# A convolution stage of a four-layer kernel: third block as a split product, statistics on ScalarE, filters' low parts spread through DRAM

## The reference

```
x = x + conv(layernorm(x), k, skip, ctx, ctx, heads=8)
x = x + experts(layernorm(x))          # 8 experts, top 2, and a shared one
x = x + attention(layernorm(x), ctx, ...)
x = x + dense(layernorm(x))
```

## Time and profile before

| | us |
|---|---|
| median of 3 runs (lowest, highest) | 3148.43 (3147.88, 3150.55) |
| the profiled execution | 3145.92 |
| its span in the trace | 3143.3 |
| PE busy in the span | 3092.0 (98%) |
| VectorE / ScalarE / GpSimd busy | 2204.3 / 1216.9 / 1154.9 |
| DMA traffic | 277.67 MB, mean 88 GB/s |

### The profile page before, as it was taken

The page is one execution under the profiler, slowest core; times in us unless marked ns, Lnnn a source line. Parts: engine busy times, 40 slices in busy tenths (PEclk is TensorE's granted clock), DMA queues, the critical chain, the costliest instruction groups (busy, mean ns, idle before and its releaser), DMA issues.

```text
span 3143.3 us, 49423 instructions
## 1 busy us (share of the span) xinstructions
PE 3092.0 (98%) x18229; PEld 2652.6 (84%) x18229; DVE 2204.3 (70%) x5733; ACT 1216.9 (39%) x2883; POOL 1154.9 (37%) x1176
## 2 busy tenths in 40 slices
PE   8999999999999899999999999999999999999999
PEld 5767676799899689999999999999998888888887
DVE  7999999755555688888888888888888433333342
ACT  3333333333444355555555555555555311111111
POOL 8988887545344332222222222222201011000010
PEclk9999999999999999999999999999999999999999
DMA  4434432279777721111111111111101200000000
GB/s 142 144 121 141 128 111 81 90 262 317 215 228 227 243 75 55 48 48 45 44 48 48 48 48 42 40 48 40 43 28 57 88 27 27 27 27 27 27 14 14
DMA packets 124973, 277.67 MB, mean 88 GB/s; under 512 B 18312, under 2 KB 18960, under 8 KB 124736
## 3 DMA queue, kind: packets, MB, share of 16 engines
q1 hardware_dynamic: 95712, 178.54, 18.0%
q0 software_dynamic: 29024, 95.97, 9.3%
HBM read 170.04 MB, written 104.42 MB: 87 GB/s over the span
## 4 chain that ended last, share of the span: by engine, by line
PE 92%; DVE 6%; DMA 1%; POOL 1%; ACT 1%; issue 0%; SPq 0%; POOLq 0%; DVEq 0%
PE f_Y L513 4%; PE g_PH L2426 4%; PE g_PH L2428 4%; PE g_PH L2427 4%; PE g_O L2442 4%; PE g_O L2441 4%; PE g_O L2440 4%; PE t_U L1704 4%; PE t_U L1705 4%; PE t_U L1706 4%; PE t_T L1680 3%; PE f_Y L519 3%; PE f_Y L521 3%; PE f_Y L518 3%; PE t_PO L1690 2%; PE t_S L1669 2%
## 5 line engine op out<-in xcount | busy, mean ns | idle before, releaser
L1830 ACT ACTIVATE t_pr<-t_sm,t_nb 128x256 f32<-128x256 f32 x512 | 256.6, 502 | 408.3 <-DVE t_nb L2037 408.3
L2211 POOL TENSOR_TENSOR t_r<-t_r 128x256 f32<-128x256 f32 x128 | 94.4, 737 | 730.7 <-DVE t_r L2016 412.7
L2498 DVE CAST g_hh<-g_hf 128x512 fp32r<-128x512 f32 x128 | 54.6, 427 | 431.0 <-PE g_O L2442 429.4
L1259 POOL TENSOR_TENSOR c_kf<-c_vt,c_ct 128x512 f32<-128x512 f32 x256 | 296.0, 1172 | 9.0 <-PE f_Y L513 9.0
L2469 ACT ACTIVATE g_hf<-g_PH,b1g 128x512 f32<-128x512 f32 x128 | 88.2, 689 | 493.8 <-PE g_PH L2428 493.8
L2047 DVE TENSOR_SCALAR t_pr<-t_pr,t_rw 128x256 f32<-128x256 f32 x512 | 239.1, 467 | 18.1
L518 PE MATMUL f_Y<-c_kh,c_th 128*128 128x512 f32 x448 | 224.5, 501 | 4.2 <-DVE c_z L976 2.6
L1704 PE MATMUL t_U<-t_voh,t_oth 128*128 128x512 f32 x512 | 202.3, 395 | 0.0
L2426 PE MATMUL g_PH<-g_xh,g_w 128*128 128x512 f32 x512 | 202.0, 395 | 0.0
L1705 PE MATMUL t_U<-t_voh,t_otl 128*128 128x512 f32 x512 | 201.6, 394 | 0.0
L1706 PE MATMUL t_U<-t_vol,t_oth 128*128 128x512 f32 x512 | 200.4, 391 | 0.0
(11 more groups left out here) (334 smaller groups left out, 9784.6 us busy)
## 6 DMA issues: line engine op xcount, KB each, us to landing
xs<-c_zero SPq DMA_DIRECT2D x71, 256.0 KB, 4.5
f_xg<-xs SPq DMA_DIRECT2D x71, 256.0 KB, 3.5
ys<-f_yt POOLq DMA_DIRECT2D x71, 256.0 KB, 3.7
f_xg<-xn SPq DMA_DIRECT2D x40, 256.0 KB, 4.9
c_xt<-x SPq DMA_DIRECT2D x32, 256.0 KB, 3.5
c_cr<-ctx SPq DMA_DIRECT2D x32, 256.0 KB, 3.9
c_ct<-ctxh SPq DMA_DIRECT2D x32, 256.0 KB, 4.4
c_t<-kt SPq DMA_DIRECT2D x32, 256.0 KB, 4.8
```

Source lines behind the costliest of these rows:

```text
L1259: gp.tensor_tensor(o, iv, ic, ALU.mult).then_inc(*GP("kv", n))
```

## The change

In words:

- Block mb = 2 is split like 0 and 1 (`if mb > 2`), so 4 plain products a head become 12 fp32r ones. Its high part is a ScalarE copy; its low part is VectorE's for u = 0 and GpSimd's for u = 1 (`low_by`).
- Statistics of both norms move from VectorE to ScalarE from head 2 on (rows of the second norm: all but the last): a Copy pass with scale -1/512 and an accumulator gives minus the mean, a Square pass with that as bias and an accumulator gives the variance; two small ones add epsilon and make the shift. Both tiles' roots lie side by side in `rsb`, and one GpSimd power serves both (`powers`).
- The filter's low part `tl` of heads 2 to 31 is no longer subtracted on GpSimd. All 32 filters (32 x 512) are loaded once (`kq`), split once into `khi` and `klo` (with 128 zeros ahead), and eight DMAs, one in each of heads 0 to 7, write 4 filters each, 128 times repeated at a pitch of 641, to DRAM (`tlt`). Read at a pitch of 640 that is the Toeplitz matrix; `load` fetches it (`tlf`), and ScalarE copies it to `tl` (`filter_lo`).
- `turned_rows`, `norm_rows`, `logit` and `best` of a head move some steps later; at the end of the loop those of head 30 move behind it. `store_xn` moves from (u=1, lb=2) of head h+1 to (u=0, lb=3) of head h+2.
- The constant `mhalf` has two columns instead of one.

The core of the diff:

```diff
@@ sync_front
+    tlw = d["tlt"].rearrange("h (p c) -> h p c", c=641)[:, :, 0:640]
+    tlr = d["tlt"][:, 128:].rearrange("h (p c) -> h p c", c=640)[:, :, 0:512]
@@ load(h)
+        if h > 1:
+            w.wait_ge(*AC["tl", h - 2 if h > 3 else -1])
+            w.wait_ge(*Q["kw"]["tlt", h // 4])
+            sp.dma_start(m.tlf[:, h % 2, :], tlr[h]).then_inc(*Q[f"u{h % 2}"]("tlf", h))
+
+    def spread_filters(c):
+        w.wait_ge(*VE["klo"])
+        w.wait_ge(*Q["kw"]["tlt", c - 1])
+        r = slice(4 * c, 4 * c + 4)
+        sp.dma_start(tlw[r], m.klo[r, :].unsqueeze(1).to_broadcast([4, 128, 640])).then_inc(*Q["kw"]("tlt", c))
...
+                if u == 0 and lb == 1 and h < 8:
+                    spread_filters(h)
                 if u == 0 and lb == 2 and h + 2 < NHC:
                     load(h + 2)
@@ conv
-            if mb > 1:
+            if mb > 2:
@@ scalar_front
+    def filters_hi():
+        w.wait_ge(*Q["kw"]["kq"])
+        copy(m.khi[:, :], m.kq[:, :]).then_inc(*AC("khi"))
+
+    def filter_lo(h):
+        w.wait_ge(*Q[f"u{h % 2}"]["tlf", h])
+        w.wait_ge(*PE["y", 8 * (h - 2) + 7])
+        copy(m.tl[:, h % 2, :], m.tlf[:, h % 2, :]).then_inc(*AC("tl", h))
+
+    def mean(h):
+        s = h % 2
+        w.wait_ge(*Q[f"x{h % 4}"]["x", h])
...
+        ac.activation(m.xn[:, s, :], m.xt[:, h % 4, :], ACT.Copy, scale=-1.0 / D, accum_out=m.ag[:, s, 0:1]).then_inc(*AC("mean", h))
+
+    def spread(h):
+        s = h % 2
+        w.wait_ge(*AC["mean", h])
+        ac.activation(m.xn[:, s, :], m.xt[:, h % 4, :], ACT.Square, bias=m.ag[:, s, 0:1], accum_out=m.ag[:, s, 1:2]).then_inc(*AC("ba", h))
+        w.wait_ge(*AC["ba", h])
+        ac.activation(root(m, h), m.ag[:, s, 1:2], ACT.Copy, scale=1.0 / D, bias=EPS).then_inc(*AC("var", h))
...
+    def mean_rows(i):
+        s = i % 2
+        w.wait_ge(*VE["out2", i])
...
@@ the loop of scalar_front, in the order of the calls within a step
                 if u == 1 and lb == 0 and more:
                     filter_hi(h + 1)
+                if u == 1 and lb == 0 and h:
+                    mean_rows(h - 1)
+                if u == 0 and lb == 0 and h and more:
+                    shift(h + 1)
                 if u == 0 and lb == 0 and more:
                     norm(h + 1)
-                if u == 0 and lb == 0 and h > 1:
-                    turned_rows(h - 2)
...
                     split(*UNITS[n])
...
+                if u == 1 and lb == 1 and h:
+                    spread_rows(h - 1)
+                if u == 1 and lb == 1 and h + 2 < NHC:
+                    mean(h + 2)
+                if u == 1 and lb == 2 and h + 2 < NHC:
+                    spread(h + 2)
+                if u == 0 and lb == 0 and h > 1:
+                    shift_rows(h - 2)
+                    norm_rows(h - 2)
                 if u == 0 and lb == 2 and h > 1:
+                    turned_rows(h - 2)
+                if u == 0 and lb == 3 and 1 <= h < LAST:
+                    filter_lo(h + 1)
+                if u == 1 and lb == 0 and h > 1:
                     logit(h - 2)
@@ vector_front
+    def filters_lo():
+        ve.memset(m.klo[:, 0:128], 0.0).then_inc(*VE("klo0"))
+        w.wait_ge(*AC["khi"])
+        ve.tensor_tensor(m.klo[:, 128:640], m.kq[:, :], f32(m.khi[:, :]), ALU.subtract).then_inc(*VE("klo"))
...
     low(0, 0, 0)
     skips(0)
+    low(0, 0, 2)
+    filters_lo()
...
-                if u == 1 and lb == 2 and h + 2 < NHC:
-                    stats(h + 2)
...
-                gather_i(h, u, lb, UNITS[n] if n < len(UNITS) and lb == 0 else None)
+                gather_i(h, u, lb, UNITS[n] if n < len(UNITS) and (lb == 0 or (lb == 2 and u)) else None)
...
-                if h and u == 1 and lb == 0:
-                    stats_rows(h - 1)
@@ gpsimd_front
+    def powers(h):
+
+        w.wait_ge(*AC["var", h + 2])
+        w.wait_ge(*AC["var0", h - 1])
+        gp.tensor_tensor(m.rsb[:, h % 2, :], m.rsb[:, h % 2, :], mhalf, ALU.pow).then_inc(*GP("rs", h + 2))
...
+                if u == 1 and lb == 3 and h < LAST:
+                    if h == 0:
+                        power(2)
+                    elif h + 2 < NHC:
+                        powers(h)
...
-                if u == 0 and lb == 1:
+                if u == 0 and lb in (1, 2):
                     low(*UNITS[n])
-                if u == 1 and lb == 0 and more:
-                    filter_lo(h + 1)
+                if u == 1 and lb == 0 and h == 0:
+                    filter_lo(1)
```

More of the change, by code:

```diff
@@ L177, in front_memory @@
     m.ob = c("ob", [8, 2, 512])
-    c("pad", [128, 3688])
+    m.tlf = c("tlf", [128, 2, 512])
+    m.khi = c("khi", [NHC, 512], F32R)
+    c("pad", [128, 104])
     sw = c("sw", [128, 8192], F32R)
@@ L342, in turn_at, with root, root_rows, filter_by @@
     return None
+def root(m, h):
+    return m.rsb[:, h % 2, 0:1]
+def root_rows(m, i):
+    return m.rsb[:, (i + 1) % 2, 1:2]
+def filter_by(K, h):
+    return K.VE if h == 0 else K.GP if h == 1 else K.AC
+def low_by(K, u, mb):
+    return K.VE if mb == 0 or (mb == 2 and u == 0) else K.GP
 def sync_front(sp, w, K):
@@ L433, in sync_front @@
                     stage_shared(h)
-                if u == 1 and lb == 2 and h:
+                if u == 0 and lb == 3 and h > 1:
+                    store_xn(h - 2)
+                if u == 1 and lb == 3 and h == LAST:
                     store_xn(h - 1)
@@ L515, in conv @@
             w.wait_ge(*AC["th", h])
-            w.wait_ge(*(GP if h else VE)["tl", h])
+            w.wait_ge(*filter_by(K, h)["tl", h])
             w.wait_ge(*AC["kh", n])
@@ L519, in conv @@
             pe.matmul(Y, m.tl[:, s, c], m.kh[:, v, mb, :], start=False, stop=False)
-            w.wait_ge(*(GP if mb else VE)["kl", n])
+            w.wait_ge(*low_by(K, u, mb)["kl", n])
             t = pe.matmul(Y, m.th[:, s, c], m.kl[:, v, mb, :], start=False, stop=mb == lb)
@@ L654, in tensor_front @@
             turn_out(LAST)
+            turn_rows(LAST - 1)
+        if n == 2:
             logit(LAST - 1)
@@ L748, in filter_hi @@
         copy(m.th[:, s, :], m.t[:, h % 3, :]).then_inc(*AC("th", h))
+    def filters_hi():
[8 more added lines that the diff above has]
+        w.wait_ge(*Q[f"x{h % 4}"]["x", h])
+        w.wait_ge(*(VE if h < 4 else AC)["nm", h - 2])
+        w.wait_ge(*VE["w", h - 2])
+        w.wait_ge(*PE["pv", h - 2])
+        w.wait_ge(*AC["xn", h - 2])
+        ac.activation(m.xn[:, s, :], m.xt[:, h % 4, :], ACT.Copy, scale=-1.0 / D, accum_out=m.ag[:, s, 0:1]).then_inc(*AC("mean", h))
@@ new lines, in spread, with shift @@
+    def spread(h):
[4 more added lines that the diff above has]
+        ac.activation(root(m, h), m.ag[:, s, 1:2], ACT.Copy, scale=1.0 / D, bias=EPS).then_inc(*AC("var", h))
+    def shift(h):
+        s = h % 2
+        w.wait_ge(*GP["rs", h])
+        ac.activation(m.nm[:, s, :], m.ag[:, s, 0:1], ACT.Copy, scale=root(m, h)).then_inc(*AC("nm", h))
@@ new lines, in mean_rows, with spread_rows @@
+    def mean_rows(i):
+        s = i % 2
+        w.wait_ge(*VE["out2", i])
+        w.wait_ge(*AC["xb", i - 2])
+        w.wait_ge(*PE["px", i - 2])
+        w.wait_ge(*Q[f"n{s}"]["nd", i - 2])
+        ac.activation(m.xb[:, s, :], m.xt[:, i % 4, :], ACT.Copy, scale=-1.0 / D, accum_out=m.ag0[:, s, 0:1]).then_inc(*AC("mean0", i))
+    def spread_rows(i):
+        s = i % 2
+        w.wait_ge(*AC["mean0", i])
+        ac.activation(m.xb[:, s, :], m.xt[:, i % 4, :], ACT.Square, bias=m.ag0[:, s, 0:1], accum_out=m.ag0[:, s, 1:2]).then_inc(*AC("ba0", i))
+        w.wait_ge(*AC["ba0", i])
+        ac.activation(root_rows(m, i), m.ag0[:, s, 1:2], ACT.Copy, scale=1.0 / D, bias=EPS).then_inc(*AC("var0", i))
@@ L750, in norm, with shift_rows @@
+    def shift_rows(i):
+        s = i % 2
+        w.wait_ge(*(GP["rs", i + 3] if i + 3 < NHC else GP["rs0", i]))
+        ac.activation(m.nm0[:, s, :], m.ag0[:, s, 0:1], ACT.Copy, scale=root_rows(m, i)).then_inc(*AC("nm0", i))
     def norm(h):
         s = h % 2
-        w.wait_ge(*VE["nm", h])
+        w.wait_ge(*(VE if h < 2 else AC)["nm", h])
         w.wait_ge(*VE["w", h - 2])
         w.wait_ge(*PE["pv", h - 2])
-        ac.activation(m.xn[:, s, :], m.xt[:, h % 4, :], ACT.Identity, scale=m.rs[:, s, :], bias=m.nm[:, s, :]).then_inc(*AC("xn", h))
+        ac.activation(m.xn[:, s, :], m.xt[:, h % 4, :], ACT.Identity, scale=root(m, h), bias=m.nm[:, s, :]).then_inc(*AC("xn", h))
@@ L790, in norm_rows @@
         s = i % 2
-        w.wait_ge(*VE["nm0", i])
+        w.wait_ge(*(VE if i == LAST else AC)["nm0", i])
         w.wait_ge(*PE["px", i - 2])
         w.wait_ge(*Q[f"n{s}"]["nd", i - 2])
-        ac.activation(m.xb[:, s, :], m.xt[:, i % 4, :], ACT.Identity, scale=m.rs0[:, s, :], bias=m.nm0[:, s, :]).then_inc(*AC("xb", i))
+        ac.activation(m.xb[:, s, :], m.xt[:, i % 4, :], ACT.Identity, scale=root_rows(m, i), bias=m.nm0[:, s, :]).then_inc(*AC("xb", i))
     def turned_rows(i):
@@ L811, in scalar_front @@
         split(*UNITS[n])
+    filters_hi()
```

(18 more changed lines are left out.)

64 lines of the change are left out of this document (28 added, 36 removed).

## The result

The changed kernel takes 3443.71 us (median of 4 runs, 3443.42 to 3446.0) against 3149.41 us: ratio 1.0943, 95% interval 1.0929 to 1.0956, 294 us slower. The forecast was 3395, and its main range, 3345 to 3465, held the time; the loss was 247 by the sum and is 294. The trace shows the mechanism that was forecast.

What follows compares the result with a forecast made beforehand. PE was taken to bound the convolution at 17.97 us a head, VectorE close behind. 3145.9 + 260.1 delay + 1.7 slow PE - 15.1 product gain = 3392.6, plus 2.5 to the median, hence 3395; 8-in-10 range 3150 to 3465.

Steps and rivals of the forecast that it cites:

- Sign and mechanism: Heads 0 to 7: slow filter chunks hold back row loads that ScalarE's statistics await; delay 260.1 us, slower at 0.82.
- The rate: Filter chunks from four SBUF rows to DRAM: 27.2 GB/s, the middle of 23.9 and 30.5, so 48.2 us for 1.31 MB.
- four rows served as by one engine: Filter chunks, lower end of the rate: 23.9 GB/s, giving 56.1 us until a chunk lands.
- the term L: Time for one filter chunk to land: 48.2 us of data plus 1.3 of landing, 49.5 us, eight times in sequence.
- The queue: SP's queue, heads 0 to 7: next head's loads stand behind a chunk, which waits for the one before; 49.5 us each.
- rival D: SP's queue: transfers behind a chunk overtake it, only 20 to 150 us slower, 3345; chance 0.02 below the main range.
- Undisturbed heads: Convolution heads without chunks: third block as 12 fp32r products saves 0.63 us a head, PE's head 17.3 us.
- rival C: Convolution heads: DMA harmless, but ScalarE's order eats the gain, 0.6 us stall a head, 3145 to 3152; chance 0.05.
- VectorE's term: VectorE per head: two statistics chains and two shifts gone, one low part added; 16.7 us falls to 15.4.
- The restart: Head 8 after the last chunk: 5.9 us from mean to PE's row turn, then 1.7 us for slow PE.
- Rivals A: Filter chunks run on four full engines, landing in 15.0 us; only the first costs, +6.6 us; 3135; chance 0.09.
- B: Filter chunks use all 16 engines with no row limit, landing in 4.7 us; 3129; chance 0.04.

Runs made afterwards that it cites:

- Experiments 1: Eleven chunk-sized DMAs alone, no computation, from differing SBUF rows, against no kernel: 1.31 MB took 53.0 us from rows 0-3, 6.1 us from all 128.
- variants 2: Changed kernel with filters reordered in SBUF so a chunk reads four rows 8 apart: 3152.18 us against 3146.37, ratio 1.0017.
- 5: Kernel before the change with only the spreading added, 4 adjacent rows a chunk; statistics and third block as they were: 3448.67 us, ratio 1.0954.
- 7: Changed kernel with a separate semaphore for each chunk, so SP does not wait for the chunk before: 3444.46 us, ratio 1.0942.
- 6: Changed kernel with the same chunks issued from ScalarE's queue at heads 0, 1, 3, 7, 11 and on: 3392.32 us, ratio 1.0776.
- variant 3: Changed kernel with each filter held four times in 128 rows, so a chunk reads 16 rows, every eighth: 3136.05 us, ratio 0.996.

## Why the prediction was right, step by step

- **Sign and mechanism: right.** The forecast took the loss from one slice of the earlier trace rows, in which a 16 KB store from eight rows moved 9.8 GB/s a busy engine. Experiments 1, 2 and 5 show it: rows on one port, nearly all of it in the spreading.
- **The rate: close, but for a reason only partly right.** "7.6 GB/s a row" is refuted; rows 0 and 1 alone give 25 GB/s. So is the other end, "four rows served as by one engine": about four were busy. What eight rows shared was two ports; halving for four rows was right by luck of the layout, for rows 8 apart it would have been wrong by a factor of nearly four. The 27.2 GB/s taken was the middle of two wrong readings, and luck in that; 1.31 MB in 53.0 us less the 2 us of a landing is 25.7.
- **The size: mis-sized in the term L.** L was 49.5 us. By itself a chunk takes 53.0, and in the kernel the chunks stand (406.96 - 74.46) / 6 = 55.4 us apart: 3.5 us from rate and landing, 2.4 between one chunk and the next. There lie the queued packets of the other transfers on the same four engines, which I had given only to the range, and SP's own issues (2.1 us after the first landing); how they share the 2.4 was not separated. Eight times 5.9 are 47, nearly the whole miss: head 9's mean starts at 463.88, not 417.8.
- **The queue: half right.** Loads wait behind a chunk; the wait between chunks adds nothing (7). "Transfers that overtake" (rival D) was priced at 3345; with a queue of their own the chunks still cost 245 us (6), part of it in SP's wait for chunk 0.
- **Undisturbed heads: right.** -0.63 a head was forecast for the products, 17.3 us; they take 17.42, -0.55. The accumulating pass that no row showed costs 0.63 us between starts (463.88, its accumulator read at 464.42, the next split at 464.51), the lower bound of 0.63 to 1.0; so rival C, the ScalarE order, did not come. The prediction had put the point where the gain is gone at 1.0 us in one place and at 1.2 in another; neither was tested. PE's waits for `c_xb` from 480 to 860 us are the same 6.4 us in three places as before. VectorE's term was wrong and did no harm: 15.4 us a head were forecast, 16.06 are busy, since some of its operations grew (`c_w` from 0.79 to 1.35 us); why was not tested.
- **The restart: right, with small errors.** From a mean to the rows ready for PE 5.9 us were forecast; at the seventh stop they are 408.26 to 413.95, 5.7 us. For the slow PE after a pause 1.7 us were forecast. At the last stop PE's row turn starts at 469.62 and the skip sum at 479.18, 9.56 us; in variant 3 the same stretch takes 7.28 (166.32 to 173.60), so it is 2.3. The place in the kernel before was put at 163.6; its trace has it at 164.5.
- **Rivals A and B** were what variants 2 and 3 are. A's 3135 would have been wrong too: it counted the chunk's bytes and not the engines' whole load. B's 3129 was 7 too good; the start loses 5 us.

## What to carry to other kernels

The time of a DMA out of SBUF depends on where its rows lie, not on its bytes alone: replicate or place the rows so that a chunk covers many ports and 16 engines (53 us became 8 for the same bytes). One slow transfer on four engines delayed every load behind it in its queue, and in another queue still cost some 30 us of the loads that use its engines; add up the load of the busiest engine, not the mean share. Where an in-order engine takes on statistics of a later head, its waits for loads become waits of all that it feeds.

## What the hardware showed unexpectedly

- SP itself stands while the queue is full of a chunk: the stage load behind chunk 0 took 17.93 us to issue and each of the next some 4.2, against 0.3 to 0.6 otherwise. Issue is a resource, too.
- Two rows are as fast as four on the same port (25 against 26 GB/s) with half the engines, so two are enough for a port. One alone was not run; an engine with a port of its own moves 24.5.
- PE's granted clock fell to 0.50 in the idle stretches of each of the eight heads (0.61 to 0.67 on the mean of each 100 us from 100 to 400). After the last stop it is still there from 465.17, where PE resumes, to 474.40:

```profile
465.17:474.40 9.23, 6.42 (x19) 4.89 (x20) 8.60 (x12) 7.16 (x15) 8.26 (x8) 0.50 0.40 117
```

Products start 0.43 us apart there instead of 0.235. While DMA set the end of a head that cost nothing that shows; after the last stop it is most of the 2.3 us above.
